# Last stage of a vision tower on one core: attention output copied out by ScalarE and added two tiles later, exponential of long tiles in two parts

## The reference, cut to what matters

```python
def _L3_ffn_ref(x, Wq_pk, pk_keys, Wq, keys_table, values_table, Wo):
    HEADS, NUM_KEYS, TOPK = 8, 64, 16
    q = (x @ Wq).reshape(b, n, HEADS, DIM) * DIM ** (-0.5)
    kv_scores, indices = _pk(x, Wq_pk, pk_keys)
    k = jnp.einsum('bnhk,bnhkd->bnhd', kv_scores, keys_table[ind])
    v = jnp.einsum('bnhk,bnhkd->bnhd', kv_scores, values_table[ind])
    sim = jnp.einsum('bihd,bjhd->bhij', q, k)
    sim = jnp.where(causal, sim, neg)
    attn = jax.nn.softmax(sim, axis=-1)
    out = jnp.einsum('bhij,bjhd->bhid', attn, v)
    return out.transpose(0, 2, 1, 3).reshape(b, n, HEADS * DIM) @ Wo
```

## Time and profile before

| | us |
|---|---|
| median of 3 runs (12518.65 to 12536.17) | 12522.75 |
| the profiled execution, its own time | 12519.97 |
| its span, first to last instruction | 12518.2 |
| TensorE busy, matmul | 9330.4 (75%) |
| VectorE busy | 8780.4 (70%) |
| ScalarE busy | 6860.9 (55%) |
| GpSimd busy | 6964.3 (56%) |
| last stage, the part looked at | 5550 to 12450 |

### The profile page before, as it was taken

The page is one execution under the profiler, slowest core; times in us unless marked ns, Lnnn a source line. Parts: engine busy times, 40 slices in busy tenths (PEclk is TensorE's granted clock), DMA queues, the critical chain, the costliest instruction groups (busy, mean ns, idle before and its releaser), DMA issues.

```text
span 12518.2 us, 138013 instructions
## 1 busy us (share of the span) xinstructions
PE 9330.4 (75%) x38094; PEld 4933.0 (39%) x38094; DVE 8780.4 (70%) x22927; ACT 6860.9 (55%) x14111; POOL 6964.3 (56%) x5848
## 2 busy tenths in 40 slices
PE   1565677476646556268888888898898888888887
PEld 1251222222223123125555445454554445454545
DVE  3633998799974875687777777777777777777761
ACT  0212444344421012167777777777777777777783
POOL 3000777587730000067777777777777777777671
PEclk9955788788766777589999999999999999999996
DMA  0000333233310000022222222222222222222220
GB/s 20 8 17 10 115 122 122 79 125 122 122 55 11 13 9 7 18 52 67 59 66 59 63 57 62 58 60 61 56 62 56 66 55 66 57 62 58 60 59 16
DMA packets 538604, 723.53 MB, mean 58 GB/s; under 512 B 412866, under 2 KB 420593, under 8 KB 503386
## 3 DMA queue, kind: packets, MB, share of 16 engines
q0 software_dynamic: 168448, 338.54, 10.4%
q1 hardware_dynamic: 369418, 376.55, 9.8%
HBM read 697.87 MB, written 8.42 MB: 56 GB/s over the span
## 4 chain that ended last, share of the span: by engine, by line
PE 30%; DVE 12%; ACT 7%; issue 4%; DVEq 4%; DMA 0%; ACTq 0%; POOL 0%
PE l3m_acc L2573 6%; PE l3m_O L2544 5%; PE l3m_S L2527 5%; PE l3m_T L2534 3%; PE l3m_DX L2563 3%; PE l3m_S L2563 2%; ACT l3m_prob L2698 2%; DVEq L2868 2%; ACT l3m_spread L2669 2%; DVE l3m_nmax L2951 1%; DVE l3m_hot L2870 1%; DVE l3m_side L2907 1%; PE l3m_T L2494 1%; PE l3m_DX L2564 1%; ACT l3m_W L2715 1%
## 5 line engine op out<-in xcount | busy, mean ns | idle before, releaser
L2469 POOL DMA_INDIRECT l3m_got<-in_l_table,l3m_row x5120 | 5051.5, 987 | 1930.6 <-issue 1082.2
L2669 ACT ACTIVATE l3m_spread<-l3m_got,l3m_weight 128x128 f32<-128x128 f32 x5120 | 2434.4, 502 | 13.7 <-DMA l3m_got<-in_l_table,l3m_row 9.6
L2573 PE MATMUL l3m_acc<-l3m_W,l3m_values 128*128 128x512 f32 x3072 | 1678.6, 628 | 198.3 <-ACT l3m_W L2715 193.1
L1325 POOL TENSOR_TENSOR m_mul<-m_st,m_wide_c 128x2048 f32<-128x2048 f32 x256 | 1159.0, 4527 | 425.5 <-DVE m_st L1598 419.8
L2707 ACT ACTIVATE l3m_probT<-l3m_T 128x512 f32<-128x512 f32 (+3 forms) x1280 | 686.4, 536 | 770.1 <-PE l3m_T L2534 761.7
L2960 DVE SCALAR_TENSOR_TENSOR tower_h<-l3m_O,l3m_pinv,tower_h 128x64 f32<-128x64 f32 x512 | 145.3, 284 | 1156.0 <-PE l3m_O L2544 1134.2
L1391 PE MATMUL m_W<-m_mul,tower_ident 128*128 128x512 f32 (+1 forms) x1536 | 809.7, 646 | 130.0 <-POOL m_mul L1325 73.7
L2544 PEld LDWEIGHTS l3m_O<-l3m_vo_g,l3m_probT 128*128 128x128 f32 x5440 | 738.3, 199 | 234.3 <-ACT l3m_probT L2707 161.4
L2534 PEld LDWEIGHTS l3m_T<-tower_ident,l3m_prob 128*128 128x128 f32 x4352 | 541.0, 151 | 681.7 <-issue 497.3
L2544 PE MATMUL l3m_O<-l3m_vo_g,l3m_probT 128*128 128x64 f32 x5440 | 751.8, 279 | 60.0 <-ACT l3m_probT L2707 59.8
L2534 PE MATMUL l3m_T<-tower_ident,l3m_prob 128*128 128x128 f32 x4352 | 770.4, 296 | 10.0 <-ACT l3m_vo_g L2690 5.7
(11 more groups left out here) (694 smaller groups left out, 19589.2 us busy)
## 6 DMA issues: line engine op xcount, KB each, us to landing
m_wide_c<-l1a_c SPq DMA_DIRECT2D x256, 1024.0 KB, 4.7
l3m_got<-in_l_table,l3m_row POOLq DMA_INDIRECT x5120
l3m_values<-in_l_table SPq DMA_DIRECT2D x288, 256.0 KB
l0i_img<-in_l_x SPq DMA_DIRECT2D x4, 1024.0 KB, 7.9
l2r_x<-l2a_hT SPq DMA_DIRECT2D x8, 512.0 KB, 5.4
qp_inw<-in_q_inw SPq DMA_DIRECT2D x1, 2336.0 KB, 7.9
l_kept<-l0t_xt,l0t_row POOLq DMA_INDIRECT x128, 2.2
l1a_c<-m_listf SPq DMA_DIRECT2D x16, 128.0 KB, 4.9
```

The lines of the kernel that those rows point to most:

```text
L1325: pool.tensor_tensor(mul[:, k % 2], st[:, k % 2], wide_c[:, k % CRING], ALU.mult).then_inc(multiplied, 1)
L2469: pool.indirect_dma_start(got[:, unit % GOT, j, :], None, table, bass.IndirectOffsetOnAxis(ap=row[:, unit // QUAD % RING, unit % QUAD, j:j ...
L2573: pe.matmul(acc[:], values[:, tile, :], W[:], start=(tile == 0), stop=(tile == TILES - 1)).then_inc(blended, 1)
L2669: copy = act.activation(spread[:, unit % 2, :, j], got[:, unit % GOT, j, :], ACT.Copy, scale=weight[:, g % RING, t, j:j + 1])
```

## The change

ScalarE copies O into a new SBUF buffer `told` of three slots (`take_O`), at the start of the next step, behind `lift`; TensorE's next first product waits for that copy and no longer for VectorE, and uses one half of O. VectorE's `scale` takes `told`, of the tile two back and no longer of the last one (`tile_at(s - 2)`; one more `scale` stands at the end). The exponential of a tile of more than 1024 keys (depth 8 to 15, 256 tiles) is made in two instructions, keys 0 to 1023 and the rest, each with a row sum of its own; VectorE adds the two sums. The scores of the next tile wait for the first part before chunk 0 and for the second before chunk 2; a tile's own transposes likewise. The wait for `grown` moves to chunk 3. `exp0` counts exponentials.

```diff
+    HALF = SEQ // 2
+    exp0 = [0]
+    for i in depth:
+        exp0.append(exp0[-1] + 1 + (i >= HALF // P))
...
-        nmax, psum, pinv = u.sb("nmax", [P, 2]), u.sb("psum", [P, 2]), u.sb("pinv", [P, 2])
+        nmax, psum, pinv = u.sb("nmax", [P, 2]), u.sb("psum", [P, LATER, 2]), u.sb("pinv", [P, 2])
+        told = u.sb("told", [P, LATER, D])
...
                 if n:
-                    pe.wait_ge(expd, n)
-                if i >= 3 * QUAD and behind:
-                    pe.wait_ge(grown, behind)
+                    pe.wait_ge(expd, exp0[n - 1] + 1)
                 pe.wait_ge(t_taken, T_at["vo", kind, g] + 1)
                 for c in range(i // 4 + 1):
+                    if n and c == 2 and depth[n - 1] >= 2 * QUAD:
+                        pe.wait_ge(expd, exp0[n])
+                    if c == 3 and behind:
+                        pe.wait_ge(grown, behind)
...
-                    pe.wait_ge(scaled, n)
+                    pe.wait_ge(o_taken, n)
                 for a in range(4 * c, min(4 * c + 4, depth[n] + 1)):
-                    last = pe.matmul(O[:, n % 2 * D:(n % 2 + 1) * D],
+                    last = pe.matmul(O[:, 0:D],
...
-                if n is not None:
-                    pe.wait_ge(expd, n + 1)
                 for c in range(turns(s)):
                     if c < chunks(s):
+                        if c % 2 == 0:
+                            pe.wait_ge(expd, exp0[n] + c // 2 + 1)
                         flip(n, c)
...
-                if n >= 2:
-                    act.wait_ge(scaled, n - 1)
+                if n >= LATER:
+                    act.wait_ge(scaled, n - LATER + 1)
                 to = (depth[n] + 1) * P
-                act.activation(prob[:, 0:to], S[:, 0:to], ACT.Exp,
-                               bias=nmax[:, n % 2:n % 2 + 1], accum_out=psum[:, n % 2:n % 2 + 1]).then_inc(expd, 1)
+                for i, lo in enumerate(range(0, to, HALF)):
+                    hi = min(to, lo + HALF)
+                    act.activation(prob[:, lo:hi], S[:, lo:hi], ACT.Exp, bias=nmax[:, n % 2:n % 2 + 1],
+                                   accum_out=psum[:, n % LATER, i:i + 1]).then_inc(expd, 1)
...
+            def take_O(n):
+                act.wait_ge(mixed, chunk0[n + 1])
+                act.activation(told[:, n % LATER, :], O[:, 0:D], ACT.Copy).then_inc(o_taken, 1)
...
                 if todo:
                     lift(todo[0])
+                if tile_at(s - 1) is not None:
+                    take_O(tile_at(s - 1))
                 part_up(mine[:1])
...
             def scale(n):
-                dve.wait_ge(expd, n + 1)
-                dve.reciprocal(pinv[:, n % 2:n % 2 + 1], psum[:, n % 2:n % 2 + 1])
-                dve.drain()
-                dve.wait_ge(mixed, chunk0[n + 1])
-                dve.scalar_tensor_tensor(h[:, at, :], O[:, n % 2 * D:(n % 2 + 1) * D], pinv[:, n % 2:n % 2 + 1],
+                dve.wait_ge(expd, exp0[n + 1])
+                sums = psum[:, n % LATER]
+                if exp0[n + 1] - exp0[n] == 2:
+                    dve.tensor_tensor(sums[:, 0:1], sums[:, 0:1], sums[:, 1:2], ALU.add)
+                    dve.drain()
+                dve.reciprocal(pinv[:, n % 2:n % 2 + 1], sums[:, 0:1])
+                dve.drain()
+                dve.wait_ge(o_taken, n + 1)
+                dve.scalar_tensor_tensor(h[:, at, :], told[:, n % LATER, :], pinv[:, n % 2:n % 2 + 1],
                                          h[:, at, :], ALU.mult, ALU.add).then_inc(scaled, 1)
...
-                before = tile_at(s - 1)
+                before = tile_at(s - 2)
                 if before is not None:
                     scale(before)
...
+            scale(QUAD * QUADS - 1)
```

More of the change, by code:

```diff
@@ L2159 @@
 COPIES = TOPK * GQ // QUADS
-GOT, RING, FREED = 4, 5, 1
+GOT, RING, FREED, LATER = 4, 5, 1, 3
 ABSENT = float(TOPK)
@@ L2412, in mix_heads @@
         scored, peaked, expd, mixed, scaled = (u.sem(n) for n in ("scored", "peaked", "expd", "mixed", "scaled"))
+        o_taken = u.sem("o_taken")
         ranked, highd, leftd = u.sem("ranked"), u.sem("highd"), u.sem("leftd")
@@ L2949, in peak @@
                 if n >= 2:
-                    dve.wait_ge(expd, n - 1)
+                    dve.wait_ge(expd, exp0[n - 1])
                 dve.tensor_reduce(nmax[:, n % 2:n % 2 + 1], S[:, 0:(i + 1) * P], AX, ALU.max,
```

## The result

The changed kernel takes 12391.99 us (median of 4 runs, 12389.59 to 12427.32) against 12520.7 of the kernel before. The forecast was 12402.

What follows compares the result with a forecast made beforehand. The prediction took TensorE to pace the last stage, idling for exponentials made late by VectorE's late row maximum. Terms -108 - 35 - 25 + 45 + 5 = -118 us from 12519.97 gave 12402 us; 8-in-10 range 12290 to 12525.

Steps and rivals of the forecast that it cites:

- the likeliest case: Whole kernel: the forecast itself, a time between 12330 and 12480 us; chance 0.62.
- Part 1: VectorE's scale two tiles later: picks start earlier, so a third of ScalarE's 323.5 us wait for the maximum goes; -108 us.
- Part 3: TensorE's clock: one long wait fewer in 32 steps, so less time at the lower clock level; -25 us.
- Part 4: ScalarE's added copy of O and second exponentials: 179 us more work, a quarter of it on the path; +45 us.
- part 5: The rest, chiefly VectorE adding two row sums in 256 tiles, counting only where the maximum is late; +5 us.
- Part 2: Exponential in two parts: TensorE's next scores start after the first part in the long tiles; -35 us.
- More goes: Rival: VectorE's head start carries from step to step and everything without a store goes, with the clock; 12263 us, chance 0.14.
- The wait only changes its name: Rival: VectorE stands at store, tail and the weights' sums as late as at scale; no change, 12520 us, chance 0.13.
- ScalarE becomes the bound: Rival: where ScalarE is behind at the first transposes, its added work lengthens the step; slower, 12561 us, chance 0.11.

Runs made afterwards that it cites:

- e1: The changed kernel with the exponential whole in one instruction, leaving only the copy of O and the later scale; 12426.96 us, ratio 0.9926 to the kernel before.
- e6: The changed kernel with a second copy of O per tile by ScalarE into a buffer nobody reads; 12386.47 us, ratio 0.9885 to the kernel before.
- e2: The kernel before with only the exponential in two parts and the scores starting on the first; 12483.2 us, ratio 0.9957 to the kernel before.
- e7: The changed kernel, but scores and transposes wait for both parts of the exponential; 12467.72 us, ratio 0.9958 to the kernel before.
- e9: The changed kernel with ScalarE copying finished quads out of acc, VectorE scaling them two steps later, and the exponential in one instruction; 12209.54 us, ratio 0.9743.

## Why the prediction was right

The forecast of 12402 us was 10 us high, within the range, and the likeliest case was the one that happened. Its parts were less exact than its sum; that the sum came this near is in part luck.

**Part 1, `scale` two tiles later, -108 (ends 0 and -158).** The mechanism was right in each point: next to no wait in `scale`, the store's wait doubled, the three maxima behind stores as late as before (10.5 us for 10.8), and in the other steps of the 32 3.9 us left of 10.3, where I had taken 7 away. What was mis-sized was the step from there to the stage and to the path. ScalarE's lateness fell by 93.5 us in e1, not 108, and by 79.0 in the change: without a store 6.4 of 10.3 us went in the 32 steps, but 84 of 177 in the stage. And of the 93.5 only 60.4 came off TensorE's wait for the exponential. The copy did not take the rest (e6). Set side by side, each late exponential and the wait of TensorE's scores that follows it, the traces show where it went: of 330.4 us of lateness before, TensorE stood through 250 at the exponential and 51 at `vo`, and 29 it never felt; in e1, of 236.9 us, 186, 45 and 6. So 23 of the 93.5 us were lateness at which TensorE was not yet waiting, and cost nothing; 6 came off the wait for `vo`. The prediction knew only the wait of the earlier trace rows.

**Part 3, the clock, -25 (0 and -50).** 39.8 us in the change and 43.3 in e1, by the busy time of the same matmuls. It made up for part of what part 1 lacked. e2, whose maxima stay late, gained nothing here: its matmuls take 6201.60 us for 6200.39.

**Part 4, ScalarE's further work, +45 (0 and +179).** The sum was near, and both terms were wrong. The copy of O was given 117 us of which a quarter, 29, on the path: it takes 53, and a second one costs nothing (e6). The second exponentials were given 62 us and so 16 on the path: they take 0.23 us each (from the start of one to that of the next instruction 1.43 us for 1152 keys in two parts, 1.20 in one), some 60 in all, as the rows had it and not 48, and some 44 of it count, with the two sums of part 5 (e7). The step that failed is "I take a quarter", one share for both: the copy stands where ScalarE waits for TensorE afterwards, the second exponential where TensorE waits for ScalarE.

**Part 2, the early start, -35 (0 and -69).** 63 us by e7, near the end of -69. The estimate compared the first part with the whole exponential in one instruction; in two, the end that it saves is 0.23 us later. Against the whole one, parts 2, 4 (second instruction) and 5 were -35 + 16 + 5 = -14 us, and measured -18 (from e1's stage to the change's) to -30 (e2's to before's), by single executions.

**The sum by experiment:** -111 (e1, with the copy) - 63 + 44 = -130, which is the stage's 129 us by construction, since each piece is a difference of two of the same stages. By the prediction's terms the same pieces were -104, -35 and +21: the misses of 28 and 23 us have opposite signs, and the sum hides them.

**The rivals.** "More goes" needed the steps with a store to go too; they did not. "The wait only changes its name" is half of what happened: VectorE's waits at the store, `tail` and the weights' sums grew by over 500 us, but in the steps without a store they held it up less than `scale` did. "ScalarE becomes the bound" falls with e6.

**What would show it.** The copy at 0.224 us, ScalarE's share of the stage at 5356.53 / 6860.40 = 78%, its wait for transposes 143 us shorter, TensorE's waits for `probT`, V and W together 1.1 us longer, far under 60: as written. Two were off: ScalarE's wait for the maximum at 251 us, not 215, and TensorE's for the exponential at 260, not 200.

## What to carry to other kernels

When a wait is taken from the front of an engine's list, follow that list to its next wait for work of the same step: in this kernel the lead lasted until there. Here an operation of every eleventh step gave it all back in that step, and the same remedy at that place (a copy by the engine that is there in time, the arithmetic later) was worth more than the change itself; with both the kernel takes 12186.66 us, faster than either. And price an added instruction by what waits behind it: the same ScalarE took 53 us more for nothing ahead of a wait of its own, and 60 us at a cost of 44 where TensorE was waiting for it.

## What was not expected of the hardware

- The duration of a short ScalarE instruction is over twice what it takes: the 128x64 copy lasts 0.224 us and the next starts 0.104 us after it. ScalarE's busy time grew by 39.8 us in e1, though copies of 112.9 us were added.
- TensorE's time for the same work went with the late maxima. The same 29368 matmuls of the stage take 6200.39 us before, 6160.56 in the change and 6084.95 in e9, with the granted clock at 0.94, 0.95 and 0.97 over the stage. In e9, whose window follows, that is 115 us of 312.

```profile
5513.10:12190.90 6677.80, 6084.95 (x29368) 3450.50 (x29367) 4957.52 (x18375) 5308.57 (x12763) 4937.79 (x4998) 0.97 0.24 61
```

- It did not go with every wait. In e2 TensorE's wait for the exponential is 37.6 us shorter than before and the matmuls take 1.2 us more; in e7 it is only 7.4 us shorter, and they take 55.3 us less. Where the two differ is ScalarE's wait for the maximum, 236.0 us in e7 and 338.0 in e2; no run changes that wait alone. The windows of e2 and e7:

```profile
5514.30:12473.40 6959.10, 6201.60 (x29368) 3500.61 (x29367) 4983.99 (x18631) 5319.92 (x12716) 4918.27 (x4994) 0.95 0.23 58
...
5525.90:12449.20 6923.30, 6145.06 (x29368) 3478.02 (x29367) 5001.07 (x18631) 5361.66 (x13228) 4901.60 (x4993) 0.95 0.23 59
```
